# Preparation in two halves with six groups of rows gathered in it, and a pair's products regrouped, in a graph-attention kernel

## The reference, cut to what matters

```python
def _L0_gnn_ref(x, edge_index, edge_attr, W_l, b_l, W_r, b_r, att, bias):
    # x: layer-normalised rows, 6250 x 256; 8 heads of 32 channels
    x_l = (x @ W_l + b_l).reshape(n, H, C)
    x_r = (x @ W_r + b_r).reshape(n, H, C)
    x_j = x_l[src]
    g = jax.nn.leaky_relu(x_r[dst] + x_j, NEG_SLOPE)
    alpha = jnp.einsum('ehc,hc->eh', g, att) + jnp.log(edge_attr)[:, None]
    # softmax of alpha over the edges of each dst, then
    out = jax.ops.segment_sum(x_j * alpha[..., None], dst, num_segments=n)
    return out.reshape(n, H * C) + bias
x = x + _L0_gnn_ref(_layernorm(x), ...)
x = x + experts(_layernorm(x))          # top 2 of 8
```

## Time and profile before

| | |
|---|---|
| three executions | 2299.76, 2302.57, 2322.25 us; median 2302.57 |
| profiled execution, first to last instruction | 1834.0 us |
| what the median has beyond that span | 468.6 us (the page gives no other time of that execution) |
| TensorE, VectorE, ScalarE, POOL busy | 93%, 77%, 68%, 71% |
| preparation, edges, rest | 0 to 151, 151 to about 1312, then routing and experts |
| stores of `kept_rows` | 7 of 896 KB, 4.4 us to landing |

### The profile page before, as it was taken

One profiled execution on the slowest core, in us unless ns is written; L12 is line 12 of the kernel. 1 busy time (PEld: TensorE's weight loads), 2 busy tenths in 40 slices (PEclk: granted clock), 3 DMA queues, 4 the chain that ended last, 5 costly groups with the idle time before them and its releaser, 6 DMA issues. The chain is left out here.

```text
span 1834.0 us, 36250 instructions
## 1 busy us (share of the span) xinstructions
PE 1704.0 (93%) x9433; PEld 1449.1 (79%) x9434; DVE 1417.0 (77%) x2670; ACT 1250.3 (68%) x3163; POOL 1299.3 (71%) x1358
## 2 busy tenths in 40 slices
PE   6895789999999999999999999998797899999998
PEld 4674578887787888788888888876596799999998
DVE  6774689999999999999999999999868433333333
ACT  3463589999898999999999999987770133233222
POOL 4866777777777777777777777776435677776775
PEclk9997899999999999999999999999857999999999
DMA  6887777877877888777878888774674344444444
GB/s 224 225 267 248 220 235 239 240 242 238 238 243 236 240 241 240 238 244 243 235 245 239 241 241 243 240 236 130 202 244 166 73 78 70 72 71 69 70 73 52
DMA packets 214752, 359.18 MB, mean 196 GB/s; under 512 B 44062, under 2 KB 103880, under 8 KB 214457
## 3 DMA queue, kind: packets, MB, share of 16 engines
q1 hardware_dynamic: 150392, 208.33, 34.9%
q0 software_dynamic: 63072, 147.92, 33.3%
q10 hardware_dynamic: 1120, 1.05, 0.2%
HBM read 302.77 MB, written 54.40 MB: 195 GB/s over the span
## 5 line engine op out<-in xcount | busy, mean ns | idle before, releaser
L829 POOL DMA_INDIRECT rows<-left_rows,idx x880 | 841.1, 956 | 269.3 <-issue 263.9
L1191 PE MATMUL p_row<-rights,hotT 128*128 128x256 f32 x1760 | 504.0, 368 | 55.4 <-issue 26.0
L1193 PE MATMUL p_row<-rows,ident 128*128 128x256 f32 x1760 | 529.8, 383 | 0.0
L1254 PE MATMUL p_gain<-W,hots 128*128 128x264 f32 x1760 | 470.4, 391 | 8.7 <-DVE acc L1029 6.3
L1191 PEld LDWEIGHTS p_row<-rights,hotT 128*128 128x128 f32 x1760 | 322.0, 192 | 131.1 <-issue 82.1
L1254 PEld LDWEIGHTS p_gain<-W,hots 128*128 128x128 f32 x1760 | 324.0, 190 | 78.9 <-issue 24.6
L1081 ACT ACTIVATE L<-p_row 128x512 f32<-128x512 f32 x440 | 259.2, 589 | 127.0 <-PE p_row L1193 125.3
L1708 ACT ACTIVATE e_hT<-e_ph,b_column 128x128 f32<-128x128 f32 x420 | 119.7, 368 | 326.0 <-PE e_ph L1733 326.0
L1000 DVE TENSOR_TENSOR W<-rows,p_weights 128x1024 f32<-128x1024 f32 x220 | 266.9, 1213 | 43.9 <-PE p_gain L1254 41.4
L1151 ACT ACTIVATE far<-iota_row,dl 128x128 f32<-128x128 f32 x880 | 299.2, 391 | 0.0
L909 DVE TENSOR_TENSOR L<-L,p_weights 128x1024 f32<-128x1024 f32 x220 | 266.1, 1210 | 27.0 <-ACT L L1081 27.0
(11 more groups left out here) (254 smaller groups left out, 1880.7 us busy)
## 6 DMA issues: line engine op xcount, KB each, us to landing
rights<-right_rows SPq DMA_DIRECT2D x440, 256.0 KB
locals<-item_locals SPq DMA_DIRECT2D x110, 256.0 KB, 3.7
rows<-left_rows,idx POOLq DMA_INDIRECT x880
right_rows<-p_parts SPq DMA_DIRECT2D x49, 256.0 KB
w<-in_L_ffn_W SPq DMA_DIRECT2D x16, 512.0 KB, 6.4
left_rows<-p_y SPq DMA_DIRECT2D x49, 132.0 KB
kept_rows<-X SPq DMA_DIRECT2D x7, 896.0 KB, 4.4
X<-kept_rows SPq DMA_DIRECT2D x7, 896.0 KB, 4.9
```

What stands on the lines that cost most here:

```text
L829: nc.gpsimd.indirect_dma_start(out=rows[:, g.slot(RINGS), n, :], out_offset=None, in_=d["left"][:, :], in_offset=bass.IndirectOffsetOnAxis ...
L1191: nc.tensor.matmul(to, hotT[:, g.slot(2), i, :], rights[:, g.slot(2), n, part * D:(part + 1) * D], start=(part == 0), stop=False)
L1193: last = nc.tensor.matmul(to, s["ident"][:, :], rows[:, g.slot(RINGS), i, 0:D], start=False, stop=True)
L1254: last = nc.tensor.matmul(p_gain[:, n, 0:D + H], hots[:, g.slot(2), i, :], W[:, g.slot(2), i, :, :].rearrange("p h c -> p (h c)"), start=( ...
```

## The change

- `prepare` runs over the tiles twice. The first pass does the left side of all 49 tiles; the transposes are written back into `X` itself. The second does the right side from there. Left and right have their own slots in `y` and `parts`, four each, and PSUM has four slots of one bank in place of two of two.
- Biases: left rows now get `b_l + bias`, right rows `b_r - bias`, so the sums over the edges carry the output bias; nodes without edges start from `bias * 1e-16` over `1e-16`. The bias addition to `X`, the seven stores to `kept_rows` go; after the edges `X` is filled from the input x (three DMAs for the last batch in place of one).
- First pass: even left tiles are copied by ScalarE and get their bias on POOL; odd ones are done by VectorE (an 8 column copy and an addition). The offsets' chain is spread over tiles 0 to 14; the 21 gathers of item rows follow from tile 16 on, src first, then dst, then weight, four in three turns of two tiles. src columns are turned at tiles 30 to 36, local columns at 41 to 47. The store of the node tiles moves from tile 12 to 16, that of the keys from 29 to 46, with the local rows behind it, which POOL casts after its last tile.
- Second pass: right and high parts on VectorE, low parts by turns on VectorE (even) and POOL (odd); weights, marks and their stores lie here. From tile 9 on POOL gathers one tile of `left_rows` after each odd low part, and the rest behind the last: 24, the groups 0 to 5. They use the semaphores of the edge stage.
- `edges`: POOL begins with group 6; indices are read from `srcs` directly, and VectorE's copy to `idx` goes. A pair's four `hotT` products come first, then one identity product of 512 columns for both items.

```diff
+EARLY_GROUPS = 6
+SRC_TURN, LOCAL_TURN, WEIGHT_TURN = 30, 41, 12
+ITEMS_READ, GATHER_AT = 16, 9
...
-                    if t + 2 < NODE_TILES:
-                        pool.wait_ge(normed, t + 3)
-                        nc.gpsimd.tensor_tensor(X[:, t + 2, :], X[:, t + 2, :], out_bias[:, :], ALU.add).then_inc(residual, 1)
...
+                for t in range(0, NODE_TILES, 2):
+                    pool.wait_ge(left_by_scalar, t // 2 + 1)
+                    nc.gpsimd.tensor_tensor(y[:, t % 4, 0:D], y[:, t % 4, 0:D], side_bias[:, 0, :], ALU.add).then_inc(left_biased, 1)
...
+                    if t >= ITEMS_READ:
+                        for i in range((t - ITEMS_READ) // 2 * 4 // 3, min(3 * QI, (t + 2 - ITEMS_READ) // 2 * 4 // 3)):
+                            read_rows(i)
+                pool.wait_ge(local_done, 1)
+                nc.gpsimd.tensor_copy(local16[:, :, :], local[:, :, :]).then_inc(local_kept, 1)
+
+                def gather(i):
+                    g, n = i // G, i % G
+                    if n == 0:
+                        pool.wait_ge(right_projected, min(NODE_TILES, -(-(g + 1) * G * DL // D)))
+                        wait(pool, gathered[g % RING], g // RING * (16 * G))
+                    gather_item(nc, d, s, g, n)
+
+                for t in range(1, NODE_TILES, 2):
+                    pool.wait_ge(right_steps, 2 * t + 2)
+                    wait(pool, right_stored[t % 4], 16 * (t // 4))
+                    nc.gpsimd.tensor_tensor(parts[:, t % 4, 1, :], right[:, t % 4, :], parts[:, t % 4, 0, :], ALU.subtract
+                                            ).then_inc(low_by_pool, 1)
+                    if t == GATHER_AT:
+                        pool.wait_ge(turned_copied, QI)
+                        for k in range(4):
+                            pool.wait_ge(left_stored[k], 16 * len(range(k, NODE_TILES, 4)))
+                    if t >= GATHER_AT:
+                        gather((t - GATHER_AT) // 2)
+                for i in range((NODE_TILES - GATHER_AT) // 2, EARLY_GROUPS * G):
+                    gather(i)
...
+                def project_left(t):
                     pe.wait_ge(x_turned_copied, t + 1)
+                    if t >= 4:
+                        pe.wait_ge(*left_copied(t - 4))
+                    multiply(t, t % 4, 0, DL, left_projected)
...
+                    if t == SRC_TURN - 1:
+                        act.wait_ge(src_in, 16 * QI)
+                        nc.scalar.activation(sf[:, :, :], rows_s[:, :, :], ACT.Copy).then_inc(cast_done, 1)
...
+                    if t == LOCAL_TURN - 4:
+                        act.wait_ge(dst_in, 16 * QI)
...
                 def gather(g):
-                    r = g.slot(RING)
-                    goals = ((weighed, g.n - (RINGS - 1)),
-                             (gathered[r], g.turn(RING) * (16 * G)),
-                             (listed, g.turn(TURN) + 1))
...
+                    if g.n >= EARLY_GROUPS:
+                        wait(pool, weighed, g.n - (RINGS - 1))
+                        wait(pool, gathered[g.slot(RING)], g.turn(RING) * (16 * G))
+                        for n in range(G):
+                            gather_item(nc, d, s, g.n, n)
...
                         for m in range(PAIR):
-                            i = PAIR * n + m
-                            to = p_row[:, n, m * D:(m + 1) * D]
                             for part in range(2):
...
+                                nc.tensor.matmul(p_row[:, n, m * D:(m + 1) * D], hotT[:, g.slot(2), PAIR * n + m, :],
+                                                 rights[:, g.slot(2), n, part * D:(part + 1) * D], start=(m == 0 and part == 0), stop=False)
+                        last = nc.tensor.matmul(p_row[:, n, :].rearrange("p (m f) -> p m f", f=D), s["ident"][:, :],
+                                                rows[:, g.slot(RINGS), PAIR * n:PAIR * (n + 1), 0:D], start=False, stop=True)
```

More of the change, by code:

```diff
@@ L167, in build @@
             pass
+        s["gathered"] = [nc.alloc_semaphore(f"g_gathered{i}") for i in range(RING)]
         s["rows"] = keep("rows", [P, RINGS, G, DL])
@@ L534, in _ @@
+                act.wait_ge(weights_done, 1)
+                nc.scalar.activation(rows_w[:, :, :], rows_w[:, :, :], ACT.Ln).then_inc(logged, 1)
+                for q in range(QI):
+                    copy_back(2 * QI + q, s["logw"])
             @block.vector
@@ L559, in reach @@
                     whole, rest = BLOCK_PARTS - 1, blocks_in(BLOCK_PARTS - 1)
-                    for own, parts in ((slice(0, P), slice(0, whole)), (slice(0, rest), slice(whole, BLOCK_PARTS))):
-                        got = ps[own, 0, 2 * parts.start:2 * parts.stop].rearrange("p (c a) -> p c a", a=2)
-                        step(nc.vector.tensor_copy(offs_column[own, parts, :], got))
-                        step(nc.vector.tensor_copy(counted[own, parts, 1:2], got[:, :, 1:2]))
+                    for own, some in ((slice(0, P), slice(0, whole)), (slice(0, rest), slice(whole, BLOCK_PARTS))):
+                        got = ps[own, 0, 2 * some.start:2 * some.stop].rearrange("p (c a) -> p c a", a=2)
+                        step(nc.vector.tensor_copy(offs_column[own, some, :], got))
+                        step(nc.vector.tensor_copy(counted[own, some, 1:2], got[:, :, 1:2]))
                     for c in range(BLOCK_PARTS):
@@ L602, in _ @@
                         step(last)
[L603 removed]
+                last.then_inc(operands_done, 1)
                 scale(0)
[L605 to L610 removed]
@@ L693, in _, with gather_item @@
                         last.then_inc(breaks_done, 1)
+def gather_item(nc, d, s, g, n):
+    i = g * G + n
+    nc.gpsimd.indirect_dma_start(
+        out=s["rows"][:, g % RINGS, n, :], out_offset=None, in_=d["left"][:, :],
+        in_offset=bass.IndirectOffsetOnAxis(ap=s["srcs"][:, i:i + 1], axis=0),
+    ).then_inc(s["gathered"][g % RING], 16)
 def node_tiles(eng, regs, s, g):
@@ L887, in _ @@
                 v.wait_ge(cleared, 2)
-                def list_sources(g):
-                    if g.c % TURN == 0:
-                        for r in range(RING):
-                            wait(v, gathered[r], (g.turn(RING) - 2) * (16 * G))
-                        nc.vector.tensor_copy(idx[:, parity(g), :], s["srcs"][:, bass.ds(g.n * G, CHUNK)]).then_inc(listed, 1)
-                def list_ahead(g):
-                    if not isinstance(g.n, int) or g.n > 0:
-                        list_sources(g)
                 def empty(g):
```

392 lines of the change are left out of this document (194 added, 198 removed).

## The result

The changed kernel took 2246.8 us (median of 4 runs, 2243.7 to 2250.3), before took 2305.0 (4 runs, 2299.8 to 2322.3): ratio 0.973, 95% interval 0.969 to 0.978, faster by some 58 us. The forecast was 2281, with a range of 2262 to 2304.

The account below looks back on a forecast made before the run. POOL's issuing of gathers was taken to pace the edge stage. Preparation +10 and edges -31 gave -21 us on 2302.6: forecast 2281 us, range 2262 to 2304.

Parts of the forecast that it names:

- The step that failed: Whole run: the 468.6 us between profiled span and median lie around the span, untouched by the change, and carry over.
- POOL's issuing is the pace of the edge stage: Edge stage: gathers start every 1.25 us, 5.0 us per group of four, and never wait on the ring of rows.
- Products, 0 us: Edges: two identity products of 512 columns replace four of 256; hidden under the gathers' 5.0 us per group, so 0.
- Early groups, -31 us: Edges: 24 gathers moved into the preparation save 30.1 us, the dropped index copy 1.4 more; bounds -20 to -33.
- The ring of 16 groups is no nearer than now: Edges: with six groups gathered early, POOL comes no closer to waiting for a free slot in the ring of rows.
- Preparation, +10 us: Before the edges: first half to 95, joint 1, second half 59, last gathers 6; sum 161 against 151.1 us.
- source and destination rows: First half of preparation: ScalarE waits about 3 us for each of the two; priced at +2 and +4 us.
- the store of the node tiles and the traffic beside it, +3: First half of preparation: the 3.5 KB store, written one word at a time, moves to tile 16; +3 us.
- Second half: Preparation's right side: POOL and VectorE alternate as the bound, 59 us (54 to 72), plus 6 for the last gathers.
- Gathers held up: Rival, preparation's second half: 20 gathers and low parts beside them each 1 us longer, +14 us; 2296 us, chance 0.17.
- The rule of the Trainium skill: Preparation's second half: a VectorE fp32 SBUF copy locks GpSimd out of writing descriptors, so it would hold up 20 gathers.
- The gathers are not the pace: Rival, edges: VectorE or TensorE need 5.0 us per group themselves; early groups bring only start-up, -6; 2307 us, chance 0.07.

Follow-up runs that it names:

- short series: A series of runs in which the unchanged kernel before takes 1837 us.
- e11: Kernel before with only a pair's identity products regrouped (two of 512 columns per group for four of 256), slow series: 2299.8 us, ratio 0.994.
- e8: Changed kernel without early groups (no gather in the preparation) and with the old order of products: 2328.0 us, ratio to before 1.008.
- e3: Changed kernel with EARLY_GROUPS = 0, all 880 gathers in the edge block and none in the preparation: 2280.1 us, ratio to before 0.987.
- long series: A series of runs in which the unchanged kernel before takes 2273 to 2313 us.
- a1: The changed kernel run again, nothing altered, in a long series: 2248.2 us, ratio to before 0.972.
- e2: Changed kernel with the old order of products (four identity products of 256 columns per group), in a short series: 1836.8 us, ratio to before 1.000.
- e14: Changed kernel with rows from group 16 on brought by SyncE's plain loads of consecutive rows instead of GpSimd's gathers, long series: 1885.4 us, before at 2272.8.

## Why the prediction was wrong

**The step that failed** is this one: "The 1834.0 us of the profiled execution lie 468.6 us under the median of 2302.6 us; nothing in the change touches what lies around the span, and I carry that difference over." It lies in the span, in the very stage that the change touches. With it fell "POOL's issuing is the pace of the edge stage": true of the earlier trace rows and of the short series, not of the runs that were timed. So the products, put at 0, were "hidden" under gathers that hid nothing.

**Products, 0 us.** Right in short series. In long ones the cover (5.0 us of gathers) is gone, and the price that I wrote for that case, 0.2 us per group and 44 us in all "in either direction", is what the runs gave in size: -0.16 to -0.21 per group, and in whole runs 13 us in before (e11) and 48 in the new kernel (e8 against e3). I had the bound and not the condition; that the size fits is partly luck, since it was 5% of a half group's 2.14 us, put there for want of a row.

**Early groups, -31 us.** In long series -34 (e3 against a1), but not as 24 x 1.253: after the block's start the first weighing comes 92 instead of 117 us later. That TensorE then has rows in hand while the completions are still late would explain it; no run tests that by itself. Its start-up in the changed kernel, ScalarE in order of time:
```profile
196.74 0.60 ACT L1138 ACTIVATE L<-p_row 128x512 f32<-128x512 f32 x1 [8.87 <-remote]
...
205.20 0.60 ACT L1138 ACTIVATE L<-p_row 128x512 f32<-128x512 f32 x1 [7.25 <-issue]
...
219.94 0.60 ACT L1138 ACTIVATE L<-p_row 128x512 f32<-128x512 f32 x1 [13.53 <-issue]
```
While GpSimd gathers without a pause (to 228 us) it waits 7 to 14 us at a time; in the 38 us without gathers, every one of the sums ScalarE waited for from 238 us on was on time. In short series, where I have the change with the old products (e2), the head start is lost again: group 6 is gathered at 178.0 instead of 186.8 us, group 16 at 235.1 (the first weighing, which frees its slot, starts at 233.6) instead of 237.8, group 36 at 337.4 instead of 337.9. "The ring of 16 groups is no nearer than now" was wrong: gathers in hand bring the ring nearer by just what they are ahead.

**Preparation, +10 us.** In long series the block starts at 173 to 177 instead of 165 and 167: about +9. The number is right by luck, as before's preparation is 14 us longer there than in its shown profile, from which I had worked; in short series it is some +25 (149.6 to 153.5 in four profiles of the old preparation against 173.7 to 177.5 in four of the new). So the span of 1813 us that I forecast was wrong in short series too: the early groups won there what the preparation lost, and the sum was 0 in place of -21. Joint of the halves: 103 instead of 95. A tile of the first half takes 1.11 us where nothing is late, as worked out; source and destination rows cost 2.6 and 3.5 us where I wrote about 3 each. Mis-sized is the store of the node tiles and the traffic beside it, +3: it is issued at 49.01 us, from 55 to 60 us the DMA engines are 98% busy at 35 GB/s, ScalarE and VectorE wait 7.7 and 8.7 us, both until 61.5, for a store of left rows, and TensorE stands still for 8.16 us. Second half: from 103.3 to the last gather before the block at 174.9, 71.6 us where I had 66: GpSimd's low part and gather cost 2.15 us per two tiles (0.72 + 0.96, and gaps of 0.3 and 0.15), not 1.95.

**The rivals.** "Gathers held up" did not happen in the preparation: of the 20 gathers behind low parts 19 took 0.96 to 0.98 us and one 1.11. In the edge block two took 2.22 us (at 190.12) and 1.88 us (at 208.92), each beside the same 1.52 us copy on VectorE as in the earlier trace rows, and in before's shown profile five gathers of 1.80 to 2.03 us lie beside its five such copies. The rule of the Trainium skill that I weighed (page "SBUF — State Buffer", section "SBUF: two separate sides") is borne out at these places, and VectorE's short steps in the second half lengthened hardly any gather. "The gathers are not the pace" was the true one (I gave it 0.07), with the wrong reason and the wrong price: it was to come from VectorE or TensorE needing 5.0 us of their own, not from late completions, and I counted its start-up and no gain per group, 2307. My argument against it, that GpSimd does not wait on the ring, is true of an execution that was not timed.

**What would show it.** The page itself showed it beforehand: a span of 1834 beside timed runs of 2300 to 2322.

## What to carry to other kernels

Compare the span with the timed runs before anything else; what lay around the span was 1.7 to 2.1 us in every other profiled execution here. Where they part by much more, the profile may be of another regime, and each cover named in the sum ("hidden by the gathers") has to be priced without it. An engine that runs ahead and then stops at a full ring can cost the others more than it gains: tying it to the consumer's progress, a few stages behind, kept its total work and took 6.5% off in a long series. Compare not only how long TensorE is idle but in what pieces, and the granted clock beside it. Rows prefetched into a ring shift the start only as far as the ring's first release allows.

## What was not expected of the hardware

In long series, and only there, TensorE's completions reach the waiting engines late, as a rule by up to 6 us in the steady part (10 at the most), 20 and 25 us in the start-up of the changed kernel (sums of 199.87 and 207.72, rectified at 219.94 and 232.53), while GpSimd gathers rows in close order, and not in the stretches of the edge stage without gathers (238 to 268 us in the changed kernel, after 300 us in e14). In a start-up with the old products one came 40 us late (e8). In the expert stage GpSimd issues indirect DMAs too, from 1900 to 2100 us of the changed kernel 54 that gather and 54 that scatter, with about 0.3 and 0.8 us between them in turn, and none of TensorE's 129 recorded updates there is over 0.7 us late; so not every indirect DMA does it. Halving the rows of a gather does not help, 0.2 us more between them does (2248 to 2141 us in two series with before at 2313): it leaves more completions over 1.5 us, but fewer long pauses of TensorE (16 over 3 us from 300 to 1200 us, 35 in a1_changed) and a clock of 0.93 instead of 0.90. Why a series is long or short, and by what path gathers hold up TensorE's semaphores, stays open: no run here tells. That the series goes with the late completions is shown, and that the gathers are needed for both (e14); that nothing else in it costs time is not, but e14 comes within 50 us of a short series.
